# A user-item graph layer on one core: three item loads on ScalarE's queue, one more warming matmul, the copy of the last 16 items on ScalarE, and all low parts of h on GpSimd

## What is computed

```python
h = item_feat @ W_item.T + b_item              # 10000 x 128
b = user_feat @ W_user.T + b_user              # user_feat is x
y = relu(adj @ h + b)                          # adj is 10000 x 10000, float32
out = layernorm(x + y)                         # over the 128 features
```

## Time and profile before

| | before |
|---|---|
| median of 3 runs | 1086.39 us |
| the profiled execution: its time, its span | 1085.97 us, 1084.1 us |
| TensorE matmul busy | 1078.3 us (99%) |
| VectorE, ScalarE, GpSimd busy | 962.1, 835.7, 115.8 us |
| DMA | 385 GB/s over the span |
| end of the lead-in (block 19's extra matmul) | 23.86 us |

### The profile page before, as it was taken

One profiled execution on the slowest core, in us unless ns is written; L12 is line 12 of the kernel. 1 busy time (PEld: TensorE's weight loads), 2 busy tenths in 40 slices (PEclk: granted clock), 3 DMA queues, 4 the chain that ended last, 5 costly groups with the idle time before them and its releaser, 6 DMA issues.

```text
span 1084.1 us, 14876 instructions
## 1 busy us (share of the span) xinstructions
PE 1078.3 (99%) x4935; PEld 901.3 (83%) x4935; DVE 962.1 (89%) x614; ACT 835.7 (77%) x801; POOL 115.8 (11%) x56
## 2 busy tenths in 40 slices
PE   9999999999999999999999999999999999999998
PEld 9888888888888888888888888888888888888888
DVE  6998898989898989898989898989898989898987
ACT  5877787878787878787878787878787878787775
POOL 4270000000000000000000000000000000000001
PEclk9999999999999999999999999999999999999999
DMA  9999999999999999999999999999999999999993
GB/s 356 419 382 420 352 422 356 422 370 423 366 422 360 422 376 423 364 422 355 423 359 422 362 423 358 423 359 422 364 422 358 421 358 422 359 422 359 419 350 154
DMA packets 66408, 417.14 MB, mean 385 GB/s; under 512 B 8194, under 2 KB 9284, under 8 KB 20052
## 3 DMA queue, kind: packets, MB, share of 16 engines
q1 hardware_dynamic: 66100, 416.68, 96.5%
q10 hardware_dynamic: 288, 0.20, 0.1%
HBM read 411.72 MB, written 5.12 MB: 385 GB/s over the span
## 4 chain that ended last, share of the span: by engine, by line
PE 99%; DVE 1%; DMA 0%; issue 0%; SPq 0%; DVEq 0%
PE acc L458 32%; PE acc L457 32%; PE acc L464 32%; PE h_ps L440 1%; PE acc L461 0%; DMA items<-item_t 0%; DVE adj_lo L722 0%; DVE h_full L679 0%; DVE stats L781 0%; PE h_ps L444 0%; SPq L335 0%; DVE items L804 0%; SPq L399 0%; DVE items L797 0%; PE z_ps L472 0%
## 5 line engine op out<-in xcount | busy, mean ns | idle before, releaser
L714 DVE TENSOR_TENSOR adj_lo<-adj,adj_hi 128x2048 fp32r<-128x2048 f32 (+2 forms) x391 | 864.8, 2230 | 106.2 <-ACT adj_hi L519 105.8
L519 ACT CAST adj_hi<-adj 128x2048 fp32r<-128x2048 f32 (+2 forms) x391 | 724.3, 1864 | 144.1 <-DMA adj<-adj_t 95.4
L457 PE MATMUL acc<-adj_hi,h_hi 128*128 128x512 f32 (+1 forms) x1580 | 604.3, 384 | 0.0
L458 PE MATMUL acc<-adj_hi,h_lo 128*128 128x512 f32 (+1 forms) x1580 | 604.3, 384 | 0.0
L464 PE MATMUL acc<-adj_lo,h_hi 128*128 128x512 f32 (+1 forms) x1580 | 417.2, 384 | 0.0
L458 PEld LDWEIGHTS acc<-adj_hi,h_lo 128*128 128x128 f32 x1580 | 296.7, 188 | 58.4
L457 PEld LDWEIGHTS acc<-adj_hi,h_hi 128*128 128x128 f32 x1580 | 296.6, 188 | 58.4
L464 PEld LDWEIGHTS acc<-adj_lo,h_hi 128*128 128x128 f32 x1580 | 292.6, 188 | 58.4
L657 POOL TENSOR_TENSOR items<-items,minus_mean 128x512 f32<-128x512 f32 x19 | 39.3, 2068 | 586.4 <-ACT minus_mean L552 586.4
L661 POOL TENSOR_TENSOR items<-items,rstd_all 128x512 f32<-128x512 f32 x19 | 37.6, 1981 | 339.9 <-ACT rstd_all L573 339.9
L544 ACT COPY gathered<-part 32x16 f32<-32x16 f32 x152 | 30.8, 203 | 22.1 <-DVE part L752 12.3
(11 more groups left out here) (51 smaller groups left out, 153.8 us busy)
## 6 DMA issues: line engine op xcount, KB each, us to landing
adj<-adj_t SPq DMA_DIRECT2D x360, 1024.0 KB, 7.7
adj<-adj_t SPq DMA_DIRECT2D x21, 512.0 KB, 5.3
adj<-adj_narrow SPq DMA_DIRECT2D x11, 952.0 KB, 7.5
xg<-x_t SPq DMA_DIRECT2D x19, 256.0 KB, 8.0
out<-items SPq DMA_DIRECT2D x19, 256.0 KB, 2.3
tail_in<-adj_tail SPq DMA_DIRECT2D x57, 32.0 KB, 4.6
adj<-item_t SPq DMA_DIRECT2D x2, 512.0 KB, 6.7
adj<-item_t SPq DMA_DIRECT2D x1, 1024.0 KB, 8.7
```

The lines of the kernel that those rows point to most:

```text
L457: nc.tensor.matmul(into, h_hi[:, k, :], high[:, c, :], start=(k == 0), stop=False)
L458: nc.tensor.matmul(into, h_lo[:, k, :], high[:, c, :], start=False, stop=False)
L519: nc.scalar.copy(into[:, places[0]:places[-1] + 1, :], source[:, places[0]:places[-1] + 1, :]).then_inc(hi_made, 1)
L714: nc.vector.tensor_tensor(into[:, places[0]:places[-1] + 1, :], source[:, places[0]:places[-1] + 1, :], high[:, places[0]:places[-1] + 1, ...
```

## The change

SyncE no longer issues loads 1, 3 and 5; ScalarE's queue issues them right behind its first transfer. `WARM` goes from 7 to 8 (14 to 16 records). The copy of the last 16 items goes from VectorE (behind the add of block 16) to ScalarE (behind its second half of `adj` tile 0, ahead of `split_h(14)`). GpSimd makes the low parts of all 20 blocks, each when its `h_hi` is there, and only then those of the pack and of W_user; `split_h_lo` and its semaphore are gone from VectorE.

```diff
--- before.py
+++ after.py
@@ -57,7 +57,7 @@
 ADJ_RING = 5
 PART_RING = 4
 H_PS_RING = 4
-WARM = 7
+WARM = 8
 
 
 OWN_SLOTS = 6
@@ -66,15 +66,13 @@
 ITEM_SLOTS = OWN_SLOTS + GUESTS
 ITEM_LOADS = ((0, 1), (1, 2), (2, 3), (3, 4), (4, 6), (6, 8), (8, 10), (10, 14), (14, 18), (18, 20))
 FIRST_ITEMS = (0, PER_TILE // 2 * P)
+ACT_LOADS = (1, 3, 5)
 ITEM_RANGES = [(max(a * PER_TILE * P, FIRST_ITEMS[1]), min(b * PER_TILE * P, N_ITEM)) for a, b in ITEM_LOADS]
 HALVES_BEFORE = 9
 HIGH_HALF_AFTER = (11, 13)
 LOW_HALF_AFTER = (13, 15)
 EARLY_BLOCKS = 16
 LATE_BLOCK_AFTER = {3: 16, 5: 17, 7: 18, 9: 19}
-TAIL_AFTER_ADD = 16
-POOL_LOWS = 9
-LOW_BLOCKS_FROM = 4
 
 
 @dataclass(frozen=True)
@@ -274,7 +272,6 @@
         w_lo_made = sem("w_lo_made")
         h_hi_made = sem("h_hi_made")
         h_lo_made = sem("h_lo_made")
-        h_lo_made_dve = sem("h_lo_made_dve")
         h_pack_made = sem("h_pack_made")
         hi_made = sem("hi_made")
         lo_made = sem("lo_made")
@@ -321,6 +318,13 @@
 
             return item_t[P * first:P * end].rearrange("(p n) -> p n", p=P)
 
+        def item_load_places(n):
+
+            first, end = ITEM_RANGES[n]
+            a = ITEM_LOADS[n][0]
+            skip = first - a * PER_TILE * P
+            return item_tiles(a, skip + end - first)[:, skip:], item_rows(first, end)
+
         block = ctx.enter_context(nc.Block())
 
         @block.sync
@@ -329,10 +333,7 @@
                 a, b = ITEM_LOADS[n]
                 if b > ITEM_SLOTS:
                     sp.wait_ge(h_product, b - ITEM_SLOTS)
-                first, end = ITEM_RANGES[n]
-                skip = first - a * PER_TILE * P
-                slots = item_tiles(a, skip + end - first)
-                sp.dma_start(slots[:, skip:], item_rows(first, end)).then_inc(item_landed[n], 16)
+                sp.dma_start(*item_load_places(n)).then_inc(item_landed[n], 16)
 
             def load_adj(g, t):
                 if later(g, 1) or t >= ADJ_RING:
@@ -401,7 +402,8 @@
                 if n == HALVES_BEFORE:
                     load_first_half(0)
                     load_first_half(1)
-                load_items(n)
+                if n not in ACT_LOADS:
+                    load_items(n)
             for t in range(1, TILES):
                 if t == BIAS_BEFORE:
                     sp.dma_start(w_user[:, :], w_user_t).then_inc(w_user_landed, 16)
@@ -485,10 +487,7 @@
                 if t == LAST:
                     pe.wait_ge(w_lo_made, 1)
                     pe.wait_ge(h_pack_made, 1)
-                if t < POOL_LOWS:
-                    pe.wait_ge(h_lo_made, t + 1)
-                else:
-                    pe.wait_ge(h_lo_made_dve, t + 1 - POOL_LOWS)
+                pe.wait_ge(h_lo_made, t + 1)
                 tile_product(0, t, 0)
             pe.wait_ge(pads_ready, 1)
             group(1, 1)
@@ -534,6 +533,16 @@
                     nc.scalar.copy(h_pack[:, :], h_tail[:, :])
                 k = t * PER_TILE
                 nc.scalar.copy(h_hi[:, k:k + n, :], h_full[:, k:k + n, :]).then_inc(h_hi_made, 1)
+
+            def copy_items_tail():
+
+                act.wait_ge(items_tail_zeroed, 1)
+                act.wait_ge(item_landed[item_load(LAST)], 16)
+                cols = (FULL - LAST * PER_TILE) * P
+                landed = item_tiles(LAST, cols + TAIL)[:, cols:cols + TAIL]
+                packs = items_tail[:, 0:len(PACKS) * PACK_LO].rearrange("p (n c) -> p n c", c=PACK_LO)[:, :, 0:TAIL]
+                nc.scalar.copy(packs, landed[:, None, :].to_broadcast([P, len(PACKS), TAIL])).then_inc(
+                    items_tail_made, 1)
 
             def gather(n):
 
@@ -603,10 +612,14 @@
                         spread_rstd(g - 1)
 
             act.dma_start(item_tiles(0, FIRST_ITEMS[1]), item_rows(*FIRST_ITEMS)).then_inc(first_items_landed, 16)
+            for n in ACT_LOADS:
+                act.dma_start(*item_load_places(n)).then_inc(item_landed[n], 16)
             for t in range(EARLY_BLOCKS):
                 split_h(t)
                 if t in HIGH_HALF_AFTER:
                     split_hi_half(HIGH_HALF_AFTER.index(t))
+                if t == HIGH_HALF_AFTER[-1]:
+                    copy_items_tail()
             for t in range(1, TILES):
                 if t == LAST:
                     act.wait_ge(w_user_landed, 16)
@@ -633,15 +646,14 @@
                                     base=0, pattern=[[-1, P]], channel_multiplier=1).then_inc(ident_ready, 1)
 
             nc.gpsimd.memset(items_tail[:, :], 0.0).then_inc(items_tail_zeroed, 1)
-            for t in range(POOL_LOWS):
+            for t in range(TILES):
                 n = full_chunks(t)
                 k = t * PER_TILE
                 pool.wait_ge(h_hi_made, t + 1)
                 nc.gpsimd.tensor_tensor(h_lo[:, k:k + n, :], h_full[:, k:k + n, :],
                                         h_hi[:, k:k + n, :].bitcast(F32), ALU.subtract).then_inc(h_lo_made, 1)
             again = slice(PACK_HI_AGAIN, PACK_HI_AGAIN + PACKED_ROWS)
-            pool.wait_ge(h_lo_made, POOL_LOWS)
-            pool.wait_ge(h_hi_made, TILES)
+            pool.wait_ge(h_lo_made, TILES)
             nc.gpsimd.tensor_tensor(h_pack[again, :], h_tail[again, :],
                                     h_pack[again, :].bitcast(F32), ALU.subtract).then_inc(h_pack_made, 1)
             pool.wait_ge(h_pack_made, 1)
@@ -679,23 +691,6 @@
                 nc.vector.tensor_tensor(h_full[:, k:k + n, :], h_ps[t % H_PS_RING][:, 0:n, :],
                                         bias_item[:, None, :].to_broadcast([P, n, HID]),
                                         ALU.add).then_inc(h_full_made, 1)
-
-            def copy_items_tail():
...
-            def split_h_lo(t):
-                n = full_chunks(t)
-                k = t * PER_TILE
-                dve.wait_ge(h_hi_made, t + 1)
-                nc.vector.tensor_tensor(h_lo[:, k:k + n, :], h_full[:, k:k + n, :],
-                                        h_hi[:, k:k + n, :].bitcast(F32), ALU.subtract).then_inc(h_lo_made_dve, 1)
 
             def split_lo(g, t):
 
@@ -829,14 +824,10 @@
             dve.wait_ge(w_bias_landed, 16)
             for t in range(TILES):
                 add_item_bias(t)
-                if t == TAIL_AFTER_ADD:
-                    copy_items_tail()
                 if t in LOW_HALF_AFTER:
                     split_lo_half(LOW_HALF_AFTER.index(t))
             for t in range(1, TILES):
                 split_lo(0, t)
-                if t >= LOW_BLOCKS_FROM and POOL_LOWS + t - LOW_BLOCKS_FROM < TILES:
-                    split_h_lo(POOL_LOWS + t - LOW_BLOCKS_FROM)
             group(1, 1)
             with dve.Fori(1, LOOP_PAIRS + 1) as i:
                 group(2 * i, 0)
```

## The result

The changed kernel takes 1091.81 us, the median of 6 runs (1090.08 to 1092.68), against 1086.31 (1086.05 to 1087.07, 6 runs). The medians differ by 5.5 us; the ratio is 1.0044, with a 95% interval of 1.0033 to 1.0055, which is 4.8 us: slower by some 5 us. The runs don't lie around their median. They form two clusters: 1090.08, 1090.28 and 1091.00, and 1092.62, 1092.64 and 1092.68.

The account below looks back on a forecast made before the run. TensorE, busy 99% of the span, was taken to bound the kernel. Lead-in -0.2, tile 1 +1.1 and tile 19 +5 gave +5.9 on 1085.97, 1091.9, and with 0.42 for the runs' median 1092.3 us; range 1086.1 to 1095.3.

Parts of the forecast that it names:

- the port: Port pair shared by VectorE instructions with two SBUF inputs and GpSimd's SBUF reads, held for a whole instruction.
- The lead-in's -0.2: Before group 0: eighth warming matmul +0.1 and the items' copy gaining 0.24, together about -0.2 us.
- The copy: Last items' copy on ScalarE: block 19's extra matmul no longer waits for VectorE; gain 0.24 us.
- the eighth warming matmul: At the start: 0.45 us long, covered by the wait for load 1 but for 0.1 us.
- Place 1, tile 1: GpSimd's blocks delay VectorE's halves and tile 1's low part; TensorE stalls 0.5 to 1.7 us, taken as 1.1.
- Place 2, tile 19: GpSimd, getting in only at VectorE's pauses, is late; TensorE stalls 2.7 to 6.6 us at tile 19, taken as 5.
- the pack's 26.05 us: GpSimd's low part of the pack, 46.75 to 72.80 us, taken as waiting for VectorE to pause.
- The sum of port work: From 18.94 to 75.42 us: 56.9 us needed at 1.24 a block, 56.5 there; doesn't fit by 0.4.
- The rival: GpSimd's blocks 9 to 13 run without pause, VectorE waits, block 18 starts 5.0 us late; 1091.2 us, chance 0.12.
- Not slower: GpSimd's blocks cost below about 1.0 us each, only the lead-in's -0.5 to +0.3 remains; 1086.1 us, chance 0.20.

Follow-up runs that it names:

- lows_back: Changed kernel with the low parts of blocks 9 to 19 given back to VectorE, the rest kept; 1086.24 us, ratio 0.9999.
- lows_alone: Kernel before with only the low parts of all blocks on GpSimd; 1090.16 us, ratio 1.0042.
- lows_zeroed: Changed kernel in which GpSimd writes zeros to the low parts of blocks 9 to 19 instead of subtracting; 1086.73 us.
- the three placements: Changed kernel, GpSimd's blocks from 9 on waiting for VectorE's first halves, for each tile, or for every second tile; 1090.88, 1090.83, 1087.92 us.
- the upper trace: Trace of the changed kernel's profiled execution, no further edit; 1092.64 us, span 1090.6.
- every_second: Changed kernel with GpSimd's blocks 9 and 10 behind VectorE's two halves, then one block for every second tile of group 0; 1087.92 us.
- after_again: Changed kernel once more, no edit; 1090.1 us over 6 runs, its trace of span 1088.0.
- series11: Kernel before with GpSimd making the low parts of blocks 0 to 10 instead of 0 to 8; 1086.59 us.
- filled: Changed kernel with 18 more matmuls of ones ahead of block 18; 1090.52 us.
- loads_alone: Kernel before with only loads 1, 3 and 5 on ScalarE's queue, WARM = 7; 1086.82 us.
- copy_alone: Kernel before with only the copy of the last 16 items moved to ScalarE; 1086.01 us.

## Why the prediction was right, and where it wasn't

**The number.** 1092.3 us was forecast and 1091.8 measured, slower by 5.5. That the two agree so well is luck: the forecast's largest term, 5 us at tile 19, never arose, and in its place stood losses of 6.5 us in one trace, most of it at block 18, and of 3.8 us in the other, at tiles 1 to 6. The median of six lies between the clusters; in the outcome of most runs the time is 1090.1, 2.2 below the forecast. What was right is the cause that the forecast was built on. The cause (GpSimd and VectorE exclude each other when both read SBUF) is shown: lows_back and lows_alone put the loss on the low parts, lows_zeroed takes away GpSimd's reads and the loss with them, and the three placements move it as the port's times say.

**The lead-in's -0.2.** Wrong in sign, small. Block 13's add came 0.5 us later in the upper trace and 0.25 in the lower, since load 4 lands later; I had looked at load 1 only. This start varies: block 13's add comes at 18.36 before and between 18.08 and 19.62 in the nine traces with the loads on two queues, so single tenths of this term mean little, and lows_back (1086.24) shows none of it in the time. The copy did what was said of it; the eighth warming matmul lay under the first loads and wasn't tried alone.

**Place 1, tile 1.** Forecast a stall of 0.5 to 1.7 after halves ending at 21.4 and 23.8 or 25.0. In the lower cluster they end at 20.95 and 24.40, and the stall is 0.75. Right, and a term of its own only in that cluster.

**Place 2, tile 19.** Wrong, and this is the step of the working that failed. I read the pack's 26.05 us as a rule: GpSimd gets in only when VectorE pauses. By that GpSimd is late and TensorE waits for it, 5 us. In both traces GpSimd's pack is through by 55 us; it gets in between VectorE's subtractions, which follow each other without a pause, one for one. What is late is VectorE's low part, at each tile in turn, and the loss is 0.58 x 5 behind tile 1 in the lower cluster. The sum of port work was mis-sized too: a block holds the port for 1.10 us, not 1.24, so all of it is 43.2 + 0.65 + 10.5 x 1.10 = 55.4 us of the 56.5 there, and fits. What doesn't fit is its order: blocks 9 to 17 are done by 40 us (the row of six ends at 40.02), though TensorE wants block 17 at 75.42 - 2 x 2.72 = 70. every_second has the same sum and loses 1.6 us instead of about 4.

**The rival** with 0.12, GpSimd keeps VectorE out, is what four of the twelve runs of the changed kernel showed by their times, and one by its trace: a gap ahead of block 18, forecast 5.0 us, measured 4.50. It was priced at 1091.2 and came to 1092.6, because the clock's fall behind the gap (1.5 us) was left out. Its account is otherwise that of the upper trace.

**Not slower** (0.20) hung on 1.0 us a block. With 1.10 the sum even fits, and the time is still slower: the sum doesn't decide, the order does.

**What stays open** is who gets the port at a boundary. GpSimd's row kept VectorE out at four boundaries in one trace and for none in after_again, lows_alone, series11 and filled. VectorE kept GpSimd's pack out for 26.05 us in the kernel before, 22.87 in series11, 23.54 in loads_alone and 26.43 in copy_alone, in the stretch where its subtractions for `adj_lo` and for `h_lo` alternate (L714 and L697 before), but let it in at the next boundary in lows_back, where they alternate too. Nothing in these traces says what settles it.

## What to carry to other kernels

Before work goes from VectorE to an idle GpSimd, look whether VectorE reads two SBUF operands in that stretch while GpSimd reads SBUF too; if so, GpSimd's idle time isn't free time, and, as here, a subtraction that cost VectorE 0.60 us costs the port 1.10. If it must be done there, space it by what the bound engine leaves (here 2.72 us a tile less 2.20), by a wait on VectorE's progress, not as early as possible. Even so it took 1.6 us more here than leaving the work on VectorE. And don't make one long row of an engine's time into a rule about who wins: another trace of the same kernel had the other outcome.

## What the runs showed that I had not expected

- Two outcomes of one program, 2.5 us apart, from one collision: VectorE's subtraction of 1.2 us took 1.74 or 6.68.
- A single-input VectorE copy (128x48, 0.18 us) stretched to 0.66 beside GpSimd's row. The prediction's sentence, that an instruction with at most one SBUF input doesn't contend, is too wide. The Trainium skill (SBUF — State Buffer, Who interferes with whom) names copies among the operations that can take the shared pair, when their operands meet its conditions. The trace of lows_alone agrees, with the 0.66 us.
- TensorE's granted clock fell to 0.5 for about 3 us after idle times of 4.50 and 2.36 us, but stayed at 1.00 after 0.76 us (series11). It cost 1.5 us the first time; the second wasn't priced.
- 0.58 us saved in the lead-in (copy_alone) was gone at tile 1 of group 0: the lead-in's end no longer sets the time there.
